# Splitting the adding DMAs of a multiscale convolution by place, moving the load and copy of x, and reordering all five engines

## The reference, cut to what matters

```
xn = layernorm(x)
q, k, v = silu(short causal convolution of 4 taps(xn @ Wq, Wk, Wv))
beta = sigmoid(xn @ Wb)
delta = delta rule in chunks (triangular inverse, running state S) of q, k, v, beta
ms = multiscale convolution of v: causal depthwise, 3, 15 and 31 taps,
     then a product by kernel_mix_w and one by channel_mixer_w
gates = softmax(gelu([xn, mean|ms|, mean|delta|, mean|v|] @ w1 + b1) @ w2 + b2)
o = rmsnorm(gates . (ms, delta, v)) * o_norm_w @ Wo
xr, xk = mixes of xn and xn of the token before
ffn = sigmoid(xr @ W_r.T) * (relu(xk @ W_k.T)^2 @ W_v.T)
out = x + o + ffn
```

## Time and profile before

| | |
|---|---|
| median of 3 runs | 3585.18 us (3582.6 to 3587.37) |
| profiled execution, its own time | 3585.26 us |
| its span, first to last instruction | 3583.2 us |
| mean granted TensorE clock | 0.987 |
| first PE instruction | 12.1 us after the start |

### The profile page before, as it was taken

The page is one execution under the profiler, slowest core; times in us unless marked ns, Lnnn a source line. Parts: engine busy times, 40 slices in busy tenths (PEclk is TensorE's granted clock), DMA queues, the critical chain, the costliest instruction groups (busy, mean ns, idle before and its releaser), DMA issues. The chain is left out here.

```text
span 3583.2 us, 97697 instructions
## 1 busy us (share of the span) xinstructions
PE 3454.6 (96%) x37184; PEld 2572.7 (72%) x37184; DVE 3199.5 (89%) x8208; ACT 2765.0 (77%) x9176; POOL 423.0 (12%) x497
## 2 busy tenths in 40 slices
PE   6999999999999999999999999999999999999986
PEld 5677777777777777777777777777777777777764
DVE  6998898998989999989999989989999998899983
ACT  5677887778887778887788877788877788777774
POOL 1011100111100111101111001111001110011110
PEclk9999999999999999999999999999999999999988
DMA  5022111122111122111221111221112221112110
GB/s 177 5 41 42 35 31 28 31 41 42 30 32 25 38 42 40 31 28 26 41 42 37 30 28 31 41 41 30 32 22 41 42 38 29 31 27 41 36 26 10
DMA packets 52204, 131.04 MB, mean 37 GB/s; under 512 B 9389, under 2 KB 9901, under 8 KB 51481
## 3 DMA queue, kind: packets, MB, share of 16 engines
q0 software_dynamic: 31744, 79.70, 12.9%
q1 hardware_dynamic: 19992, 45.10, 3.7%
HBM read 45.09 MB, written 33.55 MB: 22 GB/s over the span
## 5 line engine op out<-in xcount | busy, mean ns | idle before, releaser
L1488 DVE SCALAR_TENSOR_TENSOR my<-vT,mw,my 128x256 f32<-128x256 f32 x5408 | 2230.9, 480 | 105.6 <-ACT my L1054 69.9
L645 PE MATMUL dense<-xsh,w 128*128 128x256 f32 x2048 | 481.9, 381 | 1.3
L645 PEld LDWEIGHTS dense<-xsh,w 128*128 128x128 f32 x2048 | 368.3, 190 | 68.9 <-ACT xr L1116 8.3
L388 POOL DMA_DIRECT2D my<-prod x160 | 141.8, 886 | 964.6 <-ACT my L1054 498.4
L439 PE MATMUL front<-xsh,wk 128*128 128x256 f32 x1024 | 239.9, 387 | 3.4 <-ACT raw L835 3.4
L439 PE MATMUL front<-xsh,wv 128*128 128x256 f32 x1024 | 240.9, 388 | 0.8 <-ACT xsh L812 0.8
L586 PE MATMUL dense<-xk,wfk 128*128 128x256 f32 x1024 | 239.5, 387 | 0.0
L357 POOL TENSOR_SCALAR vare<-xsq 128x2 f32<-128x2 f32 x32 | 6.1, 192 | 1951.3 <-ACT xsh L797 1951.3
L678 PE MATMUL dense<-wo,ms 128*128 128x512 f32 x512 | 235.7, 604 | 0.0
L598 PE MATMUL dense<-wr,xr 128*128 128x512 f32 x512 | 233.7, 599 | 1.2 <-DVE xb L1471 1.2
L1065 ACT ACTIVATE prod<-vT,mw 128x256 f32<-128x256 f32 x480 | 210.3, 511 | 28.2 <-DMA my<-prod 27.9
(11 more groups left out here) (181 smaller groups left out, 6897.8 us busy)
## 6 DMA issues: line engine op xcount, KB each, us to landing
my<-prod POOLq DMA_DIRECT2D x160, 384.0 KB, 4.1
xa<-in_x SPq DMA_DIRECT2D x32, 512.0 KB, 4.2
out<-xb POOLq DMA_DIRECT2D x32, 512.0 KB, 5.9
w<-in_w SPq DMA_DIRECT2D x1, 2048.0 KB, 17.1
wv<-in_wv SPq DMA_DIRECT2D x1, 1024.0 KB, 6.6
wk<-in_wk SPq DMA_DIRECT2D x1, 1024.0 KB, 8.9
wq<-in_wq SPq DMA_DIRECT2D x1, 1024.0 KB, 8.4
wfk<-in_wfkT SPq DMA_DIRECT2D x1, 1024.0 KB, 7.1
```

Source lines behind the costliest of these rows:

```text
L388: e.dma_start(my[h % 2][:, :, :], prod[:, :, :], accum_op=ALU.add).then_inc(taps_added, 16)
L645: e.matmul(by_batch(o), w1[:, k, hs(2 * pair + c)], xsh[s % 2][:, k, :, 1:1 + P], start=(k == 0), stop=False)
L1488: i = e.scalar_tensor_tensor(o, vT[s % 2][:, c, :, off:off + P], mw[:, col:col + 1], o, ALU.mult, ALU.add)
```

## The change

The adding DMA of a round is split into three, one for each place, each with its own wait on its own product, and each place has a semaphore `taps_added[p]`. ACT's product of place p waits only for the last add into `prod[:, p, :]`, and DVE's first tap of place p only for the adds of p. `load_x` waits in addition for the adds of two steps back; `copy_x` is issued a loop turn later in SP's list and waits for the gate's matmuls of its step. The lists of PE, ACT, DVE and POOL are written anew. The amount of work stays as it was, except for 10 more DMAs a step, and whatever table loads the new order of ACT brings.

```diff
-        def adds_before(s, h, r):
-            return taps_added, 16 * (s * ADDED[H] + ADDED[h] + r)
+        def adds_before(s, h, r, p):
+            return taps_added[p], 16 * (s * ADDED[H] + ADDED[h] + r)
...
             def load_x(s):
                 if s:
                     e.wait_ge(*x_turned.upto(s - 1))
+                if s >= 2:
+                    for p in range(3):
+                        e.wait_ge(*adds_before(s - 1, 0, 0, p))
...
             def copy_x(s):
+                e.wait_ge(*gate_mm.upto(s))
...
-                if 1 <= i <= NS:
-                    copy_x(i - 1)
+                if i >= 2:
+                    copy_x(i - 2)
...
             def add_taps(s, h, r):
                 e.wait_ge(*tap_zero.upto(s, h))
-                e.wait_ge(*tap_products.upto(s, ADDED[h] + r))
-                e.dma_start(my[h % 2][:, :, :], prod[:, :, :], accum_op=ALU.add).then_inc(taps_added, 16)
+                for p in range(3):
+                    e.wait_ge(*tap_products.upto(s, 3 * (ADDED[h] + r) + p))
+                    e.dma_start(my[h % 2][:, p, :], prod[:, p, :], accum_op=ALU.add).then_inc(taps_added[p], 16)
...
             def multiply_taps(s, h, r):
-                if s or ADDED[h] or r:
-                    e.wait_ge(*adds_before(s, h, r))
                 for p in range(3):
+                    if s or ADDED[h] or r:
+                        e.wait_ge(*adds_before(s, h, r, p))
...
```

More of the change, by code:

```diff
@@ L262, in build @@
         tap_zero, taps_done = signal("tap_zero", H), signal("taps_done", 3 * H)
-        tap_products, taps_added = signal("tap_products", ADDED[H]), semaphore("taps_added")
+        tap_products = signal("tap_products", 3 * ADDED[H])
+        taps_added = [semaphore(f"taps_added{p}") for p in range(3)]
         mix_mm, mix_done = signal("mix_mm", H), signal("mix_done", H)
@@ L740, in tensor_program @@
                 if f:
+                    turn_x(i, 0)
                     turn_x(i, 1)
@@ L743, in tensor_program @@
                     inverse_W(i - 1, 1)
-                    key_state(i - 1, 1)
+                    kernel_mix(i - 1, 1)
                     inverse_Z(i - 1, 1)
-                    kernel_mix(i - 1, 1)
-                    inverse_W(i - 1, 2)
                 if f:
@@ L750, in tensor_program @@
                 if k:
-                    inverse_Z(i - 1, 2)
+                    inverse_W(i - 1, 2)
                 if f:
@@ L754, in tensor_program @@
                 if k:
-                    inverse_W(i - 1, 3)
+                    inverse_Z(i - 1, 2)
                 if f:
@@ L758, in tensor_program @@
                 if k:
+                    inverse_W(i - 1, 3)
+                if c:
+                    turn_o(i - 2, 0)
+                if k:
+                    key_state(i - 1, 1)
                     inverse_Z(i - 1, 3)
@@ L1172, in scalar_program @@
                 if c:
+                    multiply_taps(i - 2, 3, 3)
+                    copy_W(i - 2)
+                if k:
+                    take_raw_halo(i - 1, 4)
+                if c:
+                    spread_X(i - 2)
+                if k:
+                    take_raw_halo(i - 1, 5)
+                if c:
+                    join_X(i - 2)
+                    copy_tokens(i - 2, 3)
+                    scale_v(i - 2, 1)
+                    copy_half_W(i - 2)
+                if f:
+                    take_raw_halo(i, 0)
+                if k:
+                    odd_ones(i - 1)
+                if c:
                     relu_key(i - 2, 0)
-                    copy_mix(i - 2, 1)
                     square_key(i - 2, 0)
+                    scale_v(i - 2, 0)
+                    relu_key(i - 2, 1)
+                    join_half_X(i - 2)
+                    copy_mix(i - 2, 2)
+                    square_key(i - 2, 1)
+                    tanh_gate(i - 2, 0)
                 if k:
-                    short_first(i - 1, 0)
+                    short_first(i - 1, 1)
                 if c:
-                    scale_v(i - 2, 1)
-                if f:
-                    sum_x(i)
+                    copy_u(i - 2, 1)
+                    copy_u(i - 2, 0)
                 if k:
@@ new lines, in vector_program @@
+                    taps(i - 2, 3, 72, 73)
+                    taps(i - 2, 3, 67, 69)
+                    taps(i - 2, 3, 70, 71)
+                    taps(i - 2, 3, 75, 76)
+                    taps(i - 2, 3, 71, 72)
+                    taps(i - 2, 3, 73, 75)
+                    taps(i - 2, 3, 76, 78)
+                if k:
+                    short_conv(i - 1, 1)
+                if c:
+                    gate_value(i - 2, 1)
+                if k:
+                    short_conv(i - 1, 2)
+                    short_conv(i - 1, 3)
@@ L1702, in vector_program @@
                 if k:
-                    taps(i - 1, 2, 16, 17)
+                    taps(i - 1, 2, 11, 12)
+                    taps(i - 1, 2, 19, 20)
+                    mask_W(i - 1, 2)
+                    taps(i - 1, 2, 14, 15)
+                    taps(i - 1, 2, 18, 19)
+                    turn_Y(i - 1, 2)
+                    taps(i - 1, 2, 22, 23)
+                    taps(i - 1, 2, 21, 22)
+                    taps(i - 1, 2, 17, 18)
+                    taps(i - 1, 2, 20, 21)
+                    taps(i - 1, 2, 23, 25)
+                    taps(i - 1, 2, 26, 27)
                 if c:
```

429 lines of the change are left out of this document (202 added, 227 removed).

## The result

The changed kernel takes 3608.06 us (median of 4 runs, 3603.36 to 3613.22) beside 3584.73 for the kernel before on the same chip: 1.0065 times as long, 95% interval 1.0048 to 1.0082. I had said 3554 and a range that ended at 3590; the time is above it, and on the other side of no change. A steady period takes 110.0 us; 108.3 was forecast.

The account below looks back on a forecast made before the run. The prediction took PE's own work plus 1.7 us a steady period, chiefly waits for scale_B and for instructions, as the bound. It summed 3585.3 - 42 + 21 - 6 - 4 = 3554 us, range 3520 to 3590.

Parts of the forecast that it names:

- PE's waits in the new order: Steady periods: PE waits more for scale_B, turn_features, mask_W and copy_oT; +0.7 us a period, +21 us.
- Small units apart: PE's inverse stretch: projects between small units remove four fifths of the stops, taken as waits for instructions; -42 us.
- Split adds: POOL's adding DMAs in three: first place lands 0.8 to 2.8 us earlier; steady 0, bounds -0.3 and +0.5 a period.
- DVE's own bound: Steady period: DVE's work after norms_two follows without a gap, 27.0+77.8+2.3 = 107.1 us, level with PE.
- x moved: Load and copy of x on SP go off at later places, with some 30 and 40 us of cover; cost 0.
- Head: Before the steady periods: both copy_raw ahead of multiply_taps(3,1), so short_conv(0) starts some 4 us sooner; -6 us.
- Tail: After the steady periods: shorter rounds of products, and square_o(0) ahead of weighing the second half; -4 us.
- T: End of state(1), from which the forecast counted; copy_tokens(1), ahead of norms_two, was to end at T+27.0 (26.5 to 28).
- the signs of being wrong: Issue waits as before; table load before Tanh; PE waiting for scale_B over 1 us a period; kernel_mix(3) waiting for DVE.
- 4: Steady part: the gain from the stops is given back whole by DVE's lateness; 3575 to 3590 us, chance 0.11.
- 3: Steady part: ACT's chain through Gelu to norms_two and scale_B is the new bound; 3610 us, chance 0.12.

Follow-up runs that it names:

- the best kernel: Kernel before with the adding DMAs split by place and load and copy of x moved, all compute orders old: 3552.87 us, 0.9916.
- the two moves: Kernel before with split adds and x moved, plus on PE turn_beta ahead of turn_logits and turn_x(0) behind query_key(1): 3586.26 us, 1.0006.
- The spread alone: Kernel before with only PE's new order in the inverse stretch, and copy_raw(0) ahead of multiply_taps(3,1) on ACT: 3574.83 us, 0.9980.
- the third variant: Changed kernel with Silu(5) ahead of Gelu 0 on ACT, three table loads a period instead of five: 3628.33 us, 1.0117.

## Why the prediction was wrong

The sum missed by 59 us against the profiled execution (3613.2), by 54 against the median: "Small units apart" by 23, "PE's waits in the new order" by 24, head and tail by 10.

**"PE's waits in the new order", +21, is the step that failed.** It measured +45: 62 us of waits for DVE, with the 17 us for `scale_B` gone. The term was made of 39 us of waits (1.3 a period) less the old 17. What came of its parts:

| wait of PE, us in 30 periods | forecast | measured |
|---|---|---|
| `kernel_mix(0)` for `softmax_top` | nothing | 20.0 |
| `ffn_out(1)` for `gate_value(0)` | nothing | 11.8 |
| the inverse for `mask_W` and `step_Y` | 9 | 16.1 |
| `query_key(0)` and `inverse_W(0)` | 19.5 | 13.1 |
| `turn_features`, `attend(1)` | 10.5 | none |

So what failed is the two waits put at nothing. I went through the new list for late work of ACT (`scale_B`, `turn_features`, `copy_oT`) and for one unit of DVE, and these come to less than I charged, but for the inverse. The leaving of `turn_beta` from the gap ahead of `kernel_mix(0)` I didn't weigh at all: the dependence is one of a bank (logits must be read before it is written again), and the trace of before shows no wait there because the gap was covered. In the best kernel the two moves bring this wait from none to 11 us, those of `query_key(0)` and `inverse_W(0)` from 17 to 25, and cost 33 us in all. Twelve taps taken from DVE leave the waits at `kernel_mix(0)` and `inverse_W(0)` as they are, so those are a matter of what stands between, not of load. The waits for `step_Y` and `mask_W` are load in the main: six taps out take 11 us off them. `gate_value` waits 8 to 10 us even then; no run isolates its cause.

**"Small units apart", -42, was right in its mechanism and too large.** The spread alone takes the stops from 33 to 7 us. In the change they go to 11, and that is the work of two parts: with one add a round the new orders have 23 us, fewer stops (12 over 0.2 us for 33) but longer ones. The clock's dips go, 24 us at the lower level in the steady part before and none after. But PE's busy time, which I expected to fall with them, rose by 3 us, where the spread alone took 9 off it. That restarts behind the new waits cost as much is likely and not shown. The term measured -22 and +3. The Trainium skill (Runtime: NRT & Kernel Launch, "Instruction fetch mechanics") calls the crossing "mostly hidden". By count that is so here, some 270 packets in the steady part and 33 stops; but where small products stand close and a large add is in flight, PE stood up to 2.3 us, and even with the split 14 us of stops stay in the old order.

**"Split adds", 0, was wrong, on the good side.** It is worth 21 us in the old orders and 76 in the new ones. I asked how soon a third of the data lands for DVE. In the old orders I bounded that well (3 us in 30 periods, inside -0.3 to +0.5 a period) and didn't ask who else uses the DMA engines: the fetch, which is where the 21 us are. In the new orders it is DVE after all, which without the split waits 121 us for adds instead of 50. And 50 is still twice the 25 of before: the prediction let DVE's other 77.8 us of a period follow "without a gap", and 1.7 us of waits for adds stand in them, so DVE's own bound lay above the 107.1 that the prediction gave it.

So the orders are worse than the result shows: they lose 55 us on the kernel with split and x alone. On that kernel the two moves on PE lose 33 and the spread 11; DVE's load, taken from the changed kernel, gives back 17. These overlap, and 10 of the 33 are a wait for `copy_raw` that the changed kernel doesn't have. That they make up the 55 is argued, no run has the rest of the orders without the two moves, and none puts `turn_beta` and `turn_x(0)` back into the changed kernel.

**"x moved", 0:** alone it gave 8 us, 5 of them in the head, which the change as a whole doesn't keep. **"Head" and "Tail", -10:** measured 0.

**What held.** Five table loads a period, at the places named, none ahead of Tanh, and ACT at 2858 us busy for the 2850 forecast:

```profile
L881 ACT ACT_TABLE_LOAD x60 | 77.0, 1283 | 1.1
L1124 ACT ACT_TABLE_LOAD x60 | 77.0, 1283 | 1.1
L1135 ACT ACT_TABLE_LOAD x31 | 39.8, 1283 | 0.5
```

`copy_tokens(1)` ended at T+27.6 (27.0 said; its terms -1.9, +2.6 and +0.5 make +1.2, not +1.1), DVE idles 5.3 us at once ahead of `norms_two` ("near 5"), the adds land in 3.3 us on the median. DVE has lost its slack, as said. None of the signs of being wrong that the prediction named is what came: PE's main waits are at units that it didn't look at. Of the rivals, 4 had the mechanism ("the gain is given back by lateness of DVE") and not the size; 3 had the size of the time (3610) by a mechanism that the third variant speaks against.

## What to carry to other kernels

When an order is rewritten, list for each unit the pairs "engine A writes, B reads, A writes again" and what stands between them, banks of PSUM included; a unit of half a microsecond taken from such a gap can cost its cover once a period, and the trace of before shows nothing there. A gain read from one engine's stops can have its cause on a queue: before rearranging the engine, look at what is in flight when the late packet starts. And time the parts of a change one by one: here two parts were worth 30 us and the new orders lost 55.

## What the runs showed of the hardware

In the kernel before, a 16 KB instruction packet started only as a 384 KB adding DMA had ended, 9.26 us behind `turn_logits`, and PE, with products of some 10 ns, stood for 1.4 us. With the same bytes as three DMAs of 128 KB it started at 7.0 to 7.2 us in the same period, with the add still in flight. Stops at such places are 0.3 to 2.3 us long.

Three DMA issues in a row on POOL take longer than single ones, 1196 ns at the median for 860, and 128 KB land little sooner than 384, 3.3 us at the median for 4.1:

```profile
L394 POOL DMA_DIRECT2D my<-prod x480: 847/1196/1579, 55.9 to 3507.5; - x160
...
DMA to landing us min/median/max: 2.7/3.3/5.6
```
